# TensorE multiplies the identity by itself in three places behind the last convolution of a four-layer graph network

## The reference

```
x = x + attention(h, adj)     # 4 heads, masked by adj > 0.5, softmax
x = x + relational(h, adj)    # max over 7 relations of A_r (h W_r) + b
x = x + convolution(h, adj)   # relu(D^-1/2 (A + I) D^-1/2 (h W + b))
x = x + laplace(h, adj)       # layernorm, softplus(xn Ws + (I - A_norm) xn Wn)
```

## Time and profile before

| | |
|---|---|
| median of 3 runs | 698.53 us (697.9 to 700.7) |
| profiled execution | 699.71 us, its span 697.7 us |
| TensorE busy | 648.7 us, 93% |
| ScalarE busy | 544.8 us, 78% |
| VectorE busy | 531.5 us, 76% |
| GpSimd busy | 369.2 us, 53% |

### The profile page before, as it was taken

The page is one execution under the profiler, slowest core; times in us unless marked ns, Lnnn a source line. Parts: engine busy times, 40 slices in busy tenths (PEclk is TensorE's granted clock), DMA queues, the critical chain, the costliest instruction groups (busy, mean ns, idle before and its releaser), DMA issues. The chain is left out here.

```text
span 697.7 us, 20320 instructions
## 1 busy us (share of the span) xinstructions
PE 648.7 (93%) x7476; PEld 525.4 (75%) x7476; DVE 531.5 (76%) x1641; ACT 544.8 (78%) x1271; POOL 369.2 (53%) x435
## 2 busy tenths in 40 slices
PE   5669899999999999999999999999999899998855
PEld 4466778879697878788797878788796768787544
DVE  5776768887878788887878788887878778884641
ACT  5777668888888898888888897988888776865442
POOL 2545565564746565654846465655742564454420
PEclk9589999999999999999999999999999999999996
DMA  7222040222222111222222211222212210200000
GB/s 212 92 59 80 3 137 3 77 77 78 77 78 77 61 39 57 76 78 78 77 77 78 76 50 44 64 79 77 77 62 77 63 53 25 78 2 16 1 15 16
DMA packets 39532, 44.47 MB, mean 64 GB/s; under 512 B 4545, under 2 KB 23050, under 8 KB 39434
## 3 DMA queue, kind: packets, MB, share of 16 engines
q1 hardware_dynamic: 38802, 42.95, 19.7%
q10 hardware_dynamic: 632, 0.22, 0.1%
HBM read 38.83 MB, written 4.33 MB: 62 GB/s over the span
## 5 line engine op out<-in xcount | busy, mean ns | idle before, releaser
L475 POOL TENSOR_TENSOR rstd<-ve,half_neg 128x4 f32<-128x4 f32 (+1 forms) x67 | 89.1, 1329 | 208.1 <-DVE ve L1388 63.9
L797 ACT ACTIVATE side<-d_all,sd 128x512 bf16<-128x512 f32 x256 | 163.8, 713 | 35.3 <-DVE pos L1307 29.3
L1833 PEld LDWEIGHTS ps<-part,pos 128*128 128x128 bf16 x3072 | 101.3, 97 | 9.4 <-issue 6.1
L1833 PE MATMUL ps<-part,pos 128*128 128x66 bf16 x3072 | 103.4, 193 | 0.2 <-DVE pos L1307 0.2
L1307 DVE TENSOR_TENSOR pos<-side,none 128x2048 bf16<-128x2048 bf16 x64 | 80.7, 1260 | 6.1 <-ACT side L797 5.1
L1369 DVE TENSOR_REDUCE best<-ps 128x128 f32<-128x896 f32 x64 | 68.5, 1086 | 12.8 <-PE ps L1929 11.4
L2031 PE MATMUL ps<-u,adj_tr 128*128 128x128 f32 x512 | 62.5, 282 | 3.0 <-ACT u L897 3.0
L2031 PEld LDWEIGHTS ps<-u,adj_tr 128*128 128x128 f32 x512 | 60.6, 198 | 4.3 <-ACT u L897 4.3
L1819 PEld LDWEIGHTS ps<-part,nmask 128*128 128x128 bf16 x1536 | 53.4, 99 | 13.1 <-issue 12.9
L1877 PE MATMUL ps<-adj_tr,h 128*128 128x512 f32 x128 | 58.5, 600 | 0.2 <-ACT h L706 0.2
L1891 PE MATMUL ps<-adj_in,h 128*128 128x512 f32 x128 | 57.8, 593 | 0.0
(11 more groups left out here) (162 smaller groups left out, 1488.0 us busy)
## 6 DMA issues: line engine op xcount, KB each, us to landing
adj_in<-in_adj SPq DMA_DIRECT2D x16, 1024.0 KB, 5.8
d_all<-d_dram SPq DMA_DIRECT2D x64, 256.0 KB, 3.7
x_in<-in_x SPq DMA_DIRECT2D x16, 256.0 KB, 3.0
out_y<-y_out SPq DMA_DIRECT2D x15, 256.0 KB, 2.5
d_dram<-sd_t SPq DMA_DIRECT2D x64, 2.0 KB, 1.4
w_sb<-in_L_gnn_W SPq DMA_DIRECT2D x7, 64.0 KB, 2.2
b_sb<-in_L_gnn_b SPq DMA_DIRECT2D x1, 256.0 KB, 3.2
out_y<-y_out SPq DMA_DIRECT2D x2, 128.0 KB, 1.8
```

Of the source, the lines that this page charges most:

```text
L475: G.tensor_tensor(rstd[:, cut], ve[:, cut], half_neg[:, cut], ALU.pow).then_inc(power, 1)
L797: last = A.activation(side[:, t, :], d_all[:, h, :], ACT.Sign, bias=sd[:, 0, h, t:t + 1])
L1833: last = mm(ps[:, B_HEADS[q] + i // 2, o:o + VAL], pos[h % 2][:, t, i * P:(i + 1) * P], parts[n][:, t, h, :], start=False, stop=(i % 2 == ...
```

## The change

Three groups of matmuls are added to TensorE's order. Each product has the identity as its stationary and as its moving operand, is 128x128 in f32, and is written to the first 128 columns of PSUM bank 0; nothing reads it. 44 stand behind the last `conv_product`, 16 between the two `z_transposed`, and 6 behind the second. Ahead of the first group stands a wait on `best_ok` for 64.

```diff
+            def idle_products(count, b):
+
+                for _ in range(count):
+                    mm(bank(b)[:, 0:P], ident[:], ident[:], start=True, stop=True)
+
...
             conv_product(final(0))
             conv_product(final(1))
+            pe.wait_ge(best_ok, final(0).whole(T))
+            idle_products(44, B_H0T)
             z_transposed(final(0))
+            idle_products(16, B_H0T)
             z_transposed(final(1))
+            idle_products(6, B_H0T)
             laplace_linear(final(0))
             laplace_linear(final(1))
             laplace_product(final(0))
```

## The result

The median with the change is 702.19 us (701.69 to 703.07, 9 runs), against 698.53 (697.33 to 702.02, 9 runs) before. The ratio of the runs is 1.0044, 95% interval 1.003 to 1.0058: slower by 3.1 us (2.1 to 4.1), just inside the 0.5% (3.5 us) that counts as no change. The forecast was 700.9 (698.8 to 703.0). The two medians lie further apart than the ratio says, 3.7 us or 0.52%.

A forecast was written before the change was run, and what follows sets the result against it. Before, a chain through VectorE, POOL, ScalarE and TensorE set the end. Fills delaying laplace_linear 5.50 us, less 3.51 from full clock, put laplace(0) 1.99 later: 700.5 to 701.7 us, forecast 700.9, range 698.8 to 703.0.

The forecast's parts named there:

- The count of passes: Each added f32 product on TensorE is two passes, so 66 products are 132: 88, 32 and 12.
- The price of a pass: A 128x128 f32 pass on TensorE at full clock costs 0.1116 us, a product 0.223 us.
- The bound: Between last convolution and laplace_linear, TensorE becomes the bound; the fills put laplace_linear back by 5.50 us.
- What the clock gives back: From laplace_linear to laplace(0), full clock instead of half takes 4.78 us instead of 8.29: 3.51 us returned.
- The wait on best_ok: Ahead of the first fill, the wait costs nothing: best_ok reaches 64 13 us before TensorE arrives.
- The turning point: Time is lost if fills delay laplace_linear over 3.51 us: above 0.0965 us a pass or some 57 products.
- The clock elsewhere: TensorE's clock in the kernel before was read as full speed everywhere but at the two ends.
- From the profile to the median: From a profiled 701.7 us, the run median's 1.18 lower gives 700.5; set a little above, at 700.9.
- a TensorE which never idles would repeat better: Some of the 697.9 to 700.7 us spread before may be clock changes, which a never idle TensorE avoids.
- One pass a product: Rival, 4%: a product takes 0.11 us, all fills end inside their gaps, laplace(0) 3.84 us earlier, 694.7 us.
- The clock did not fall during products of the identity: Answers a rival, 4%: clock falls at 677.0 during the first fill, laplace_linear 15.6 us late, 714 to 715 us.
- seams: Rival, 14%: 0.12 us a pass and 0.1 to 0.2 us at six joins between fills and waits, 702.6 us.

The follow-up runs named there:

- the control: Kernel after without products in the three places, 16 behind the last laplace_product, wait kept; run twice: 698.82 us (ratio 0.9999) and 700.37 us (1.0006).
- the third profile of before: Kernel before, nothing changed, profiled once more in a single run: 700.33 us.

## Why the prediction was right

*The count of passes.* Right: 132 records. The overrun hangs on it, and the experiment with transposes, one pass each, shows what the other count would have given: 696.2 instead of 702.2.

*The price of a pass.* 0.1116 was forecast; 88 in 682.82 - 672.99 = 9.83 us are 0.1117, and doubling gives 0.1117.

*The bound.* TensorE became it, as forecast: the fills put laplace_linear back by 5.50 us. ScalarE's zt and z of half 1 were hidden under the second fill.

*What the clock gives back.* 3.51 was forecast, 3.59 it was (8.29 - 4.70), against an execution of before in which the clock returned late; against one like the first profile of the control it would be less. Half the products get the same without the overrun, which is shown by a run.

*The wait on best_ok.* It cost nothing: the first product stands 0.22 us behind t0, the spacing of two passes.

*The turning point.* By the prediction's own sum, 681.65 + 3.51 - 671.97 = 13.19 us over 136 passes, it is 0.0970 us a pass and not 0.0965; nothing rests on it.

*The clock elsewhere.* The prediction took the clock to be full everywhere but at the two ends. The line of 40 slices was too coarse for that: between 40 and 100 us it is 0.91 on average in that trace. That lies far ahead of t0 and does not touch the steps behind it.

*From the profile to the median.* This is the term that was sized too small. The sum gave +1.99 and I added 0.4 for the runs of before whose clock might behave otherwise; the ratio says 3.1 (2.1 to 4.1). That the median still fell into the range, and the ratio inside the 0.5%, is in part luck. One reason is shown: the same steps without the fills can end 1.7 us earlier than in the profile. At one execution in five, as in the profiles, that would be an estimated 0.35 us on average, about what was added. The rest of the 1.1 us is open; it may be more early returns, something ahead of t0, or the interval. The argument that a TensorE which never idles would repeat better does not hold up: the 9 runs with the change spread over 1.4 us and those of before over 4.7, but the 4 runs with twice the products, where TensorE hardly idles either, spread over 3.4.

*The rivals.* One pass a product did not occur; its price, 3.84 us less than before in the profile, was nearly that of the version with half the products (3.76). The clock did not fall during products of the identity. The fills had no seams: from the two transposes to the fill behind them it is 0.21 and 0.22 us, two passes.

## What to carry to other kernels

Work put on an engine only to keep its clock up must be counted in passes as the trace counts them, and must end before the instruction that it stands ahead of could start; here 33 products gain 0.4% and 66 lose about as much. It takes all three gaps, and enough in each: with 22 products in the first alone, with 8 and 3 in the other two alone, and with 11, 4 and 2 in all three, the clock fell somewhere in the profile, and no gain can be told from none. Where the clock falls and returns in a stretch, one profile is one draw of several; compare several, and count from an event near the stretch.

## What I had not expected of the hardware

The clock can fall after TensorE has gone back to work: with only the first fill it fell at 687.35, 1.07 us into laplace_linear. In the kernel before and the control, with the same idle stretch behind t0, it fell anywhere from t0+2.4 (at 674.5 in the third profile of before) to t0+5.2, and was back from t0+14.2 (the control) to t0+19.5 (691.6, again in the third profile of before, whose rows are these):

```profile
674.00:675.00 1.00, 0.00 (x0) 0.00 (x0) 0.93 (x6) 0.00 (x0) 0.00 (x0) 0.75 0.33 99
691.50:692.00 0.50, 0.50 (x6) 0.50 (x5) 0.00 (x0) 0.47 (x2) 0.00 (x0) 0.93 0.00 0
```

The runs of one kernel spread over 1.4 us (the change, 9 runs) to 6.0 us (only the first 44 products, 10 runs). What sets the spread is not shown.
